# A graph network on one core: raw rows gathered by index for every second group of edges, from the prepare block on, and the first centring on VectorE

## The reference

```python
h = relu(layernorm(x))
Wh = h @ W + b                                  # layer 1
Wr, Wc = Wh[src], Wh[dst]
sim = sum(Wr * Wc) / max(|Wr| * |Wc|, 1e-8)
base = edge_weight * softplus(deg_coeff[0] * edge_weight_n2 + deg_coeff[1]) * (src != dst)
x = x + scale * (c0 * segment_sum(base * relu(sim) * Wc, src)
               + c1 * segment_sum(base * -relu(-sim) * Wc, src) + c2 * Wh)
h = relu(layernorm(x))                          # layer 2
msgs = mlp(concat(h[dst], h[src]))
x = x + mlp(concat(h, segment_sum(msgs, dst)))
```

## Time and profile before

| | us |
|---|---|
| median of 3 runs | 2582.36 |
| lowest and highest | 2574.97, 2586.78 |
| the profiled execution's own time | 2563.28 |
| its span, first to last instruction | 2561.5 |
| PE, DVE, ACT, POOL busy in it | 1723.2, 1549.9, 848.9, 1599.2 |

### The profile page before, as it was taken

The page is one execution under the profiler, slowest core; times in us unless marked ns, Lnnn a source line. Parts: engine busy times, 40 slices in busy tenths (PEclk is TensorE's granted clock), DMA queues, the critical chain, the costliest instruction groups (busy, mean ns, idle before and its releaser), DMA issues. The chain is left out here.

```text
span 2561.5 us, 52835 instructions
## 1 busy us (share of the span) xinstructions
PE 1723.2 (67%) x13575; PEld 1408.5 (55%) x13575; DVE 1549.9 (61%) x5934; ACT 848.9 (33%) x3238; POOL 1599.2 (62%) x1364
## 2 busy tenths in 40 slices
PE   3664766666666666676660038787778777877999
PEld 2444656666656566565650026666656666666444
DVE  6884756666666666566664935554544445456677
ACT  3772323323223232232322722222222222222665
POOL 5884888888888888888887654444444444441333
PEclk9986555555555555555555558887888788788999
DMA  3774544544445445454533753333323323331676
GB/s 116 257 246 135 119 86 84 91 90 86 92 81 94 84 90 92 85 92 82 91 49 90 248 147 92 73 81 72 75 71 80 71 72 72 76 78 29 198 210 188
DMA packets 355054, 273.07 MB, mean 107 GB/s; under 512 B 94672, under 2 KB 298528, under 8 KB 354976
## 3 DMA queue, kind: packets, MB, share of 16 engines
q1 hardware_dynamic: 271530, 233.22, 31.1%
q0 software_dynamic: 81536, 38.61, 14.2%
q10 hardware_dynamic: 1910, 0.37, 0.1%
HBM read 206.69 MB, written 65.34 MB: 106 GB/s over the span
## 5 line engine op out<-in xcount | busy, mean ns | idle before, releaser
L1290 POOL DMA_INDIRECT x<-e_sums,e_to x392 | 628.8, 1604 | 146.1 <-issue 115.1
L934 POOL DMA_INDIRECT e_near_source<-h,e_near_ids x392 | 388.3, 990 | 450.9 <-DVE e_near_ids L947 320.4
L1527 PE MATMUL bank<-e_window,e_onehot 128*128 128x64 f32 x2352 | 526.8, 423 | 167.2 <-DVE e_onehot L1315 132.0
L1527 PEld LDWEIGHTS bank<-e_window,e_onehot 128*128 128x128 f32 x2352 | 509.0, 331 | 186.3 <-issue 126.3
L1044 PE MATMUL bank<-e_near_to_edge,e_near_window 128*64 128x128 f32 x2352 | 219.1, 296 | 255.7 <-DMA e_near_window<-h 149.3
L1265 POOL DMA_INDIRECT e_ends<-wh,e_ids x296 | 289.5, 978 | 101.2 <-issue 100.9
L1575 PE MATMUL bank<-e_parts,e_same 128*128 128x64 bf16 x2940 | 177.5, 241 | 230.7 <-DVE e_parts L1384 129.4
L1044 PEld LDWEIGHTS bank<-e_near_to_edge,e_near_window 128*64 128x64 f32 x2352 | 166.5, 151 | 291.9 <-DVE e_near_to_edge L955 149.4
L1575 PEld LDWEIGHTS bank<-e_parts,e_same 128*128 128x128 bf16 x2940 | 166.5, 131 | 249.2 <-issue 249.2
L1017 ACT ACTIVATE e_near_hid<-bank,mb_col 128x512 f32<-128x512 f32 x98 | 67.3, 687 | 628.4 <-PE bank L1064 379.4
L968 DVE TENSOR_TENSOR e_near_msgs<-bank,mb_row 128x256 f32<-128x256 f32 x98 | 41.3, 421 | 322.9 <-PE bank L1072 209.3
(11 more groups left out here) (173 smaller groups left out, 3301.5 us busy)
## 6 DMA issues: line engine op xcount, KB each, us to landing
e_window<-wh SPq DMA_DIRECT2D x392, 96.0 KB
e_near_window<-h SPq DMA_DIRECT2D x392, 96.0 KB
e_owners<-ends SPq DMA_DIRECT2D x98, 256.0 KB
n_x<-x SPq DMA_DIRECT2D x98, 256.0 KB, 3.1
n_x<-in_x_dram SPq DMA_DIRECT2D x49, 256.0 KB
wh<-n_wh SPq DMA_DIRECT2D x49, 256.0 KB
x<-n_x SPq DMA_DIRECT2D x49, 256.0 KB
e_rel<-rel SPq DMA_DIRECT2D x98, 128.0 KB
```

The lines of the kernel that those rows point to most:

```text
L934: pool.indirect_dma_start(out=t.source[s][:, j, :], out_offset=None, in_=tabs["h1"], in_offset=bass.IndirectOffsetOnAxis(ap=t.ids[s][:, j: ...
L1290: pool.indirect_dma_start(out=added_tab, out_offset=bass.IndirectOffsetOnAxis(ap=t.to[s][:, j:j + 1], axis=0), in_=t.sums[s][:, j, :], in_ ...
L1527: last = nc.tensor.matmul(bank[FIND_BANKS[s]][:, j * D:(j + 1) * D], onehot, window, start=w == 0, stop=w == WK - 1)
```

## The change

Four things are changed.

- **Which groups are ahead.** Every second group from group 3 on (3, 5, ..., 95) is gathered raw, 47 instead of 24. Group 1 and group 97, and the even ones, are gathered from `wh` (204 DMAs instead of 296). GpSimd's step of the edge stage issues two rows' gathers instead of three, for the groups in slots 0 and 2, and then the scatter as before. The ahead work of the edge stage comes every second group, on two sets of buffers instead of one, and its mean is folded into the centring.
- **When they are gathered.** 14 of the 188 raw gathers are issued in `prepare`: `src` is loaded, cast, turned and copied to `edge_i` ahead of the other three arrays, behind semaphores of its own. The rest come in node phase 0, four for each block: two behind a wait for `xc_ready` and a step of a semaphore (`paced`), two behind a wait for `h_ready` and a step.
- **The first centring** goes from GpSimd to VectorE: one operation, total x (-1/64) + x, which also replaces the mean. It stands behind `add_x` in the step.
- **SPLIT** is 4 instead of 5: ScalarE makes four rows of h, VectorE four.

Also the hardware loop of layer 1's edge stage ends one round earlier (`plain`), and that round is written out.

```diff
-AHEAD = ESLOTS - 1
+AHEAD_FIRST, AHEAD_EVERY = 3, 2
-AHEADS = GROUPS // ESLOTS
+EARLY = 14
+AHEADS = (GROUPS - 1 - AHEAD_FIRST) // AHEAD_EVERY
...
+def gather_ahead(pool, c, x, start, end):
+    for n in range(start, end):
+        pool.indirect_dma_start(
+            out=c["ahead"][:, n // G, n % G, :], out_offset=None, in_=x,
+            in_offset=bass.IndirectOffsetOnAxis(
+                ap=c["edge_i"][:, 0, AHEAD_FIRST + AHEAD_EVERY * (n // G), n % G:n % G + 1], axis=0),
+        ).then_inc(c["ahead_in"], 16)
...
+                pool.wait_ge(src_taken, 1)
+                for n in range(0, EARLY, 2):
+                    pool.sem_inc(src_paced, 1)
+                    gather_ahead(pool, c, x, n, n + 2)
...
-    def pool_centre(self, pool, s, k):
-        pool.wait_ge(self.mean_ready, count(s, k))
+    def dve_centre(self, dve, s, k):
+        dve.wait_ge(self.total_ready, count(s, k))
...
+        self.nc.vector.scalar_tensor_tensor(rows(self.xc[s][:]), by_row(self.total[s][:]), -1.0 / D, rows(self.x[s][:]),
+                                            ALU.mult, ALU.add).then_inc(self.xc_ready, 1)
...
-    SPLIT = R // 2 + 1
+    SPLIT = R // 2
...
-        rounds_of_blocks(dve, [(-2, squares), (0, mean), (-6, add_x), (-2, normed)])
+        rounds_of_blocks(dve, [(-2, squares), (0, total), (-6, add_x), (0, centre), (-2, normed)])
...
-        gather_ahead(0, 6)
+        share = -(-(AHEADS * G - EARLY) // BLOCKS)
         for n in range(BLOCKS):
-            ln.pool_centre(pool, n % SLOTS, n // SLOTS)
-            gather_ahead(6 + 8 * n // 5, 6 + 8 * (n + 1) // 5)
-        gather_ahead(6 + 8 * BLOCKS // 5, len(rows_ahead))
+            start = EARLY + share * n
+            pool.wait_ge(ln.xc_ready, n + 1)
+            pool.sem_inc(paced, 1)
+            gather_ahead(pool, c, x, min(start, AHEADS * G), min(start + share // 2, AHEADS * G))
+            pool.wait_ge(ln.h_ready, n + 1)
+            pool.sem_inc(paced, 1)
+            gather_ahead(pool, c, x, min(start + share // 2, AHEADS * G), min(start + share, AHEADS * G))
...
     def gather(s, k):
         if layer == 0 and near:
-            last = isinstance(k, int) and k * ESLOTS + s == GROUPS - 1
-            share = AHEAD * G // ESLOTS
-            for n in range(share * s, G * (s + 1) if last else share * (s + 1)):
-                gather_rows(n // G, k, n % G)
+            for n in range(2 * s, 2 * s + 2):
+                gather_rows(AHEAD_EVERY * (n // G), k, n % G)
+            if s % AHEAD_EVERY and not t.is_ahead(s, k, near):
+                for j in range(G):
+                    gather_rows(s, k, j)
```

More of the change, by code:

```diff
@@ L161, in build @@
         )
-        prepare(nc, c, tabs, src, dst, edge_weight, edge_weight_n2, W, b, deg_coeff, coeff_param,
+        early = ExitStack()
+        c["ahead"] = early.enter_context(nc.sbuf_tensor("ahead", [P, AHEADS, G, D], FP32))
+        prepare(nc, c, tabs, x, src, dst, edge_weight, edge_weight_n2, W, b, deg_coeff, coeff_param,
                 scale_param, mW1, mb1, mW2, mb2, uW1, ub1, uW2, ub2)
-        first_phases(nc, c, tabs, x, sb)
+        first_phases(nc, c, tabs, x, sb, early)
         c["sems"] = Semaphores(nc)
@@ L438, in rounds_of_blocks @@
         steps(k)
-    with eng.Fori(first, full) as k:
+    with eng.Fori(first, full - plain) as k:
         steps(k)
-    for k in range(full, full + first + 1):
+    for k in range(full - plain, full + first + 1):
         steps(k)
@@ L588, in vector, with total, centre @@
     def vector(dve):
-        def mean(s, k):
+        def total(s, k):
             ln.dve_total(dve, s, k)
-            ln.dve_mean(dve, s, k)
+        def centre(s, k):
+            ln.dve_centre(dve, s, k)
         def squares(s, k):
@@ L1197, in end_rows, with is_ahead @@
         return self.ends[s][:, j, end, :]
-    def is_ahead(self, s, near):
-        return near and self.layer == 0 and s == AHEAD
+    def is_ahead(self, s, k, near):
+        among = not isinstance(k, int) or 0 <= ESLOTS * k + s - AHEAD_FIRST < AHEAD_EVERY * AHEADS
+        return near and self.layer == 0 and s % AHEAD_EVERY == AHEAD_FIRST % AHEAD_EVERY and among
     def all_gathered(self, eng, s, k, near):
-        if self.is_ahead(s, near):
-            eng.wait_ge(self.ahead.copied, k + 1)
+        if self.is_ahead(s, k, near):
+            eng.wait_ge(self.ahead.copied, self.ahead.nth(s, k, AHEAD_FIRST) + 1)
             return
-        eng.wait_ge(self.gathered[s], 16 * G * (1 if near else 2) * (k + 1))
+        times = 1 if near and self.layer == 0 and s % AHEAD_EVERY else k + 1
+        if near and self.layer == 0 and s % AHEAD_EVERY and k:
+            times = 2
+        eng.wait_ge(self.gathered[s], 16 * G * (1 if near else 2) * times)
 def same_block(j, i):
```

146 lines of the change are left out of this document (77 added, 69 removed).

## The result

The changed kernel takes 2627.48 us (median of 4 runs, 2614.45 to 2633.75); the kernel before, on the same chip, took 2584.57 (4 runs, 2574.97 to 2589.03). The ratio is 1.018, with a 95% interval of 1.012 to 1.023. It is slower by about 43 us, where I had forecast 56 us faster, and it lies outside my range. The interval leaves out 1, so the loss is real; whether it is more than 2% it doesn't say. The profiled execution has 2626.74 us and a span of 2625.0.

What follows compares the result with a forecast made beforehand. GpSimd's issue of indirect DMAs was taken to bound layer 1's edge stage. Terms of -117.8, +28 and +34 us summed to -56, from 2582.4 to 2526 us; range 2482 to 2578.

Steps and rivals of the forecast that it cites:

- Gathers taken out: Layer 1's edge stage: 92 gathers of `wh` go, taking 117.8 us off GpSimd's path.
- fewer gathers between scatters: Edge stage: less cover for the scatters' landing, a wait of 0.35 us in each of 97 groups, 34 us.
- the hidden landing: Rival, edge stage: the scatters' landing stays covered, so the 34 us don't come; 2492 us, chance 0.17.
- the scatters' chain: Rival, edge stage: four scatters and a landing become the bound, 123 us of waits; 2615 us, chance 0.10.
- my rival's 1280: Rival, phase 0: raw gathers slow to 1.28 us each beside VectorE, 57 us on the path; 2583 us, chance 0.03.
- the blocks come faster than that, so it waits no more: Phase 0: GpSimd needs about 5.2 us per block and never waits after the first pairs; raw gathers end at 262 us.
- GpSimd hides all of it: Phase 0: GpSimd, ending at 262 us, covers VectorE's added time; last stores at about 232, or 251 at worst.
- an edge stage that starts after 275: Sign listed as showing the forecast wrong; first edge gather was forecast at about 262 us, first scatter at about 283.
- That wait disappears: End of phase 0: the 11.22 us between GpSimd's last raw gather and first edge gather, spent until stores are done, goes.
- VectorE's price: Phase 0: the centring on VectorE costs 0 to 0.60 us a block, 0 to 29 us in all, taken as 10.
- The start of the edge stage: Windows and one-hots are ready, product at 269 us, first scatter 14 us later at 283; 28 us later than before.
- Nothing of this (a clock or fetch effect elsewhere): Rival: the result comes from none of the named effects but from a clock or fetch effect elsewhere; chance 0.04.

Runs made afterwards that it cites:

- e8: The changed kernel, with GpSimd waiting at each block of node phase 0 until the four raw gathers of the block before have landed; 2638.9 us.
- f6: The kernel before with the centring on VectorE alone, h split as before (five rows VectorE, three ScalarE); 2588.8 us.
- f1: The changed kernel, with GpSimd waiting for its landed gathers at every second block of phase 0, so eight stand in a row; 2585.9 us.
- f3: The kernel before, with GpSimd in layer 2 waiting after two of a group's four gathers until these two have landed; 2431.6 us beside 2587.0.
- h4: The changed kernel, with GpSimd waiting at each block of phase 0 until three of the last four gathers have landed; 2588.6 us.
- h3: The kernel before, with GpSimd in layer 2 waiting behind a group's second gather only until the first has landed; 2409.8 us.
- k2: The changed kernel with h split 5 to 3, a short stop at every second block of phase 0 and a short stop in layer 2; 2451.2 us.

## Why the prediction was wrong, step by step

**Right.** *Gathers taken out* and *fewer gathers between scatters*: -118 + 34 = -84 was forecast for the stage, -79 measured. The landing wait came as read from the packets: the mean idle time before the first scatter of a group is 0.75 us and was 0.41, so +0.34 for my 0.35. The period of a group is 10.7 us for my 10.6. The rivals of the hidden landing and of the scatters' chain both fall with that. The early gathers run from 8.32 to 25.95 us, as forecast, and cost nothing. The raw gathers did not get slow (1008 ns for my rival's 1280), so the Trainium skill's rule (SBUF — State Buffer, Who interferes with whom) that VectorE can lock GpSimd out doesn't show in them; what acted runs the other way, from GpSimd to the rest.

**The step that failed** is "the blocks come faster than that, so it waits no more", and with it "259" and "262". Both halves were right by their rows: a gather in a row takes 1.28 us, and blocks without a hold-up come every 3.26 to 3.96 us. I had joined them as if the engines were independent. GpSimd was to run behind, in one row of 172 gathers, and a row holds the others up. That is a feedback: they stand until GpSimd has caught up and must wait for them, 3.7 us in the median and at most 4.8; then the next row starts. So phase 0 ran neither at GpSimd's pace (5.1 us a block) nor at its own (3.96), but at (333.3 - 41.6) / 48 = 6.1 us, and "GpSimd hides all of it" had no GpSimd ahead or behind to hide anything. The last block's stores ended at 345 us; I had said 232, or 251 at worst. The sign was in my own list ("an edge stage that starts after 275"). `e8` shows the size: with stops the same engines end at 228.

**"That wait disappears"**: it grew, from 11.22 to 31.22 us, as GpSimd's gathers ended at 313.9 and the last stores at 345.

**VectorE's price.** The 0 to 29 us held the truth, for the wrong reason. I priced VectorE's centring; it adds nothing to a block (`f6`). I wrote that "ScalarE's fourth row of h lies beside it"; it lies on the loop, 0.24 us a block, 12 us in all, and TensorE's clock adds up to 0.45. The row for it was in the profile: before, too, ScalarE's only idle time in a block is the one for the turn. I had taken VectorE for the bound because its busy share was the highest.

**The start of the edge stage.** The term of 14 us from VectorE's product to the first scatter held: it is 14.7 (363.04 to 377.69). What failed is "Windows and one-hots will be ready this time". I had 7 us from the first gather to the product, and it took 18.0, as before (17.9). The windows are rows of `wh`, so they can't be loaded until the last stores are done, and now the stores, not GpSimd, were last. Where the windows were there long before, in `e8` and `f1`, it took 6.6 and 6.7 us to the product and 17.1 from there, 24 in all. The twelve gathers of this start, in a row, also hold up the others: ScalarE goes on at 362.0, 1.6 us behind the row, though TensorE's products were done at 358.9, and SyncE needs 7.69 us to issue four window loads beside the row and 3.61 just behind it.

**The rivals.** All four were about queues and prices that I could see. "Nothing of this (a clock or fetch effect elsewhere)", with 0.04, is what came. I gave it no mechanism, though the trace of before had one to be found: ScalarE stood twice, 5 and 7 us, in the row of 14 gathers at the end of phase 0, and 22 times in 600 us of layer 2.

**Still open**: by what path a row of gathers holds up ScalarE. It is not the number in flight, the bytes or GpSimd's being busy. It isn't the loading of instructions either, as far as the packets show: from 177 to 320 us, with six of the 14 waits, only q0 (GpSimd's gathers) and q1 (the other DMAs) move anything. Rows of four show no waits in phase 0 (`e8`) and do in layer 2; why was not tried. Neither was the edge stage, where scatters stand between the gathers: between the first scatter and the last, the kernel before has two such waits over 3 us in one trace and 15 in the other, with 1122 and 1123 us for the stage, and the changed kernel has none.

## What to carry to other kernels

Don't move gathers into a stage because GpSimd has time there: first look at what the other engines do in the trace while GpSimd issues several indirect DMAs in a row. Idle times of 5 to 10 us whose releaser had been done long before, nearly all ending within a microsecond or two of GpSimd's last gather, are the sign; then a wait of GpSimd behind every four gathers, even of its own making, can be worth far more than it costs (here 155 us in layer 2). How many gathers and how long a stop has to be tried in each stage: in phase 0 the stops brought the change no further than level with the kernel before. And a stage's bound is the loop whose instructions follow without a gap, not the engine with the highest busy share.

## What the runs showed of the hardware

- While GpSimd issues gathers 0.30 us apart, ScalarE, and in layer 2 VectorE too, stand although what they wait for is done, and in rows of eight TensorE's eight matmuls at L1054 take 3.4 us instead of 0.60. In rows of twelve after the change ScalarE's wait begins 8.2 to 8.5 us into the row and ends within some 2 us of its end. GpSimd busy with fills 130 us of 130 does nothing of the kind.
- Behind the end of a gather's issue its landing releases GpSimd after 2.3 us (median of 84 stops in `f3`). The Trainium skill (Perfetto Trace Analysis, Per-instruction lifecycle: what the profiler-reported window actually captures) says that the profile's end of such a DMA is the end of its descriptors' making and not of the data's movement; the 2.3 us agree.
- A semaphore step or a memset of one column between pairs of gathers does not part a row; a wait that isn't met does, of 1.9 to 2.9 us behind four in phase 0 (`e8`, `h4`). In layer 2, stops of 1.1 us between rows of mostly two went with 2409.8 us (`h3`, one run); behind eight in phase 0, 1.5 us was too short (`k2`).
- TensorE's turn of four 128x128 tiles is waited for 0.77 us at a granted clock of 1.0 (2.4 GHz) and 1.22 us at 0.5 (1.2 GHz).
